# Attention on one core: V products in pairs of key tiles, exponentials per head, and other work between all scores

## The chip, the core and the metric

The kernel runs on one core of a Trainium2 chip. The metric is the device time of the whole program in microseconds, the median of several executions.

## What is computed

The reference is one layer on x of shape (4, 1024, 128): a layer norm, then attention and a gated feed-forward in parallel, both added to x.

```python
xn = _layernorm(x)
# attention: HEADS 16, KV_HEADS 8, DIMS 64, scale = (64 / 16) ** -0.5
xq = rope(q @ Wq); xk = rope(kv @ Wk); xv = kv @ Wv
xk = jnp.repeat(xk, 2, axis=-1); xv = jnp.repeat(xv, 2, axis=-1)
scores = jax.nn.softmax(xq @ xk * scale, axis=-1)
out = (scores @ xv) ... @ Wo
# feed-forward: h = silu(x @ wg.T) * (x @ wu.T); out = h @ wd.T, 384 wide, weights from int
x = x + attn(xn) + ffn(xn)
```

Everything is float32. Since every key and value column is repeated twice, the kernel works with 32 instead of 64 rows per head; for the scores it splits numbers into a rounded part and a rest (`hi`, `lo`), 3 x 32 = 96 rows deep, and takes two more rows for the maximum that is subtracted.

## The kernel before

The feed-forward, the layer norm and the first projections come first, until about 110 us; the rest, which this case is about, is attention. It goes over 4 batches and 4 groups of 4 heads (16 steps), and in each over two halves of the 512 queries: 32 slots, numbered u. Slot u works on four things at once, in program order on each engine, with semaphores between them and no scheduler:

- the scores of slot u: 8 key tiles (kt) of 128 keys, 4 heads (h) each. `score(kt, h)` is one matmul 98 x 512 into `bank_s[:, h % 2]`, so there are two banks, and a score waits for the exponential that read its bank. ScalarE takes the exponential into `prob[:, kt % RING, h]`, a ring of four key tiles. `pv` multiplies a key tile's four heads with V into `bank_o`, four matmuls 32 columns wide, one for each head.
- the row maxima of slot u + 1: 16 tiles, `max_tile` (two matmuls into two of the four `scores` banks), each reduced by VectorE (L824); a tile waits until the reduction of the tile two before has ended. After the 16th, VectorE splits them (`split_max`, the cast L830 and L832), TensorE transposes them, ScalarE reads them and SyncE's queue stores them into the packed queries.
- the projection of slot u + 4 (`project`, four chunks of three matmuls into `scores`, and `project_v`, 12 small matmuls), rotated by VectorE (`rotate`, six operations), rounded by ScalarE and subtracted by GpSimd for slot u + 3 (`round_hi`, `split_lo`). The first two maximum tiles of the next slot wait until the rotation has left the `scores` banks.
- the denominators of slot u - 1 and its output: GpSimd sums the exponentials of key tiles 0 to 6 (`add_probs`, five operations over 2048 elements, L1011 and L1018), VectorE adds tiles 4 and 5 ahead of that (`pair_sum`, L917), in place in `prob`. TensorE multiplies by ones (`denominators`, L404 and L407), transposes (L414), VectorE inverts, ScalarE spreads, TensorE transposes back (L421), VectorE multiplies (`normalise`), TensorE projects with Wo (`project_out`, L430, for slot u - 2), ScalarE reads, GpSimd adds (`add_out`).

Slots 0 to 3 and 28 to 31 are written out, the 24 between are a loop over 4 slots. The last four slots have no projection, the last has no maxima. `prob_ready` counts NE = 3 exponentials for each key tile: heads 0 and 1 together (L768), then 2 and 3 (L779).

Of the kernel before, what the change touches and what calls it, by code (L numbers as in the profile page):

```python
# [69 lines left out]
NE = 3  # L70

EXP_OF = [0, 0, 1, 2]

INVERT_AFTER = 13


def build(nc, x, tables, w_qkv, wo_even, wo_odd, w_gu, w_down, ident_in, out):
# [10 lines left out]
    with ctx:  # L88
# [27 lines left out]
        wgu = keep("wgu", [128, 2, 2 * HT, 128], F32R)  # L116
        wdn = keep("wdn", [128, HT, D])
# [20 lines left out]
        prob_sum = keep("prob_sum", [128, 2, HG, HALF])  # L138

# [208 lines left out]
        def _(pe):  # L348
# [16 lines left out]
            def project_v(w, t, w_from=w_stage, x_from=x_stage):  # L365

                for j in range(QT):
                    at = t * HALF + j * 128
                    for n, (a, r) in enumerate(((0, 0), (1, 0), (0, 1))):
                        last = mm(bank_m[:, j * 128:(j + 1) * 128], x_from[:, r, at:at + 128], w_from[:, a, 4, :],  # L370
                                  start=n == 0, stop=n == 2)
                last.then_inc(proj_ready, 1)
# [159 lines left out]
            def slot(i, j, t, last_pair):  # L532
# [36 lines left out]
                for kt in range(KT):  # L569
                    score(kt, 0)  # L570
                    score(kt, 1)

                    if kt in (0, 3, 4):
                        maxima()
                        pv_before(kt)
                    elif kt < 6:
                        pv_before(kt)
                        maxima()
                    else:
                        if not last_pair:  # L580
                            if kt == 6:

                                pe.wait_ge(max_read, TILES * (v + 1))
                            project(2 * (kt - 6), w, t, s + 2)
                        pv_before(kt)
                    score(kt, 2)
                    if kt in (3, 4):
                        maxima()
                    score(kt, 3)

                    if kt in (0, 1, 2, 3):
                        maxima()
                    if kt == 0:
                        maxima()
                    elif kt == 1:
                        if not is_second(u):
                            project_out(u - 2, 1 - j, s - 1)
                        maxima()
                    elif kt == 2:
                        if not is_first(u):  # L600
                            denominators(u - 1, 1 - t)
                        maxima()
                    elif kt == 4:
                        if not is_first(u):
                            transpose_den(u - 1)
                        maxima()
                    elif kt == 5:
                        if not is_first(u):
                            transpose_inv(u - 1)
                    elif kt == 6:  # L610
                        if do_max:

                            at_least(pe, o_done, u)
                            transpose_max(v)
                        if not last_pair:
                            project(1, w, t, s + 2)
                    elif kt == 7 and not last_pair:
                        project(3, w, t, s + 2)
                        pe.wait_ge(maxT_read, v + 1)
                        project_v(w, t)  # L620
# [6 lines left out]
            pairs_of_steps(pe, body)  # L627
            pv(UNITS - 1, KT - 1, 1)
# [8 lines left out]
        def _(act):  # L637
# [109 lines left out]
            def slot(i, j, t, last_pair):  # L747
# [3 lines left out]
                for kt in range(KT):  # L751

                    if not (first and kt < RING):
                        act.wait_ge(pv_done, 8 * u + kt - 3)
                        if kt == 0:
                            act.wait_ge(sum_done, 5 * u - 1)
                        elif kt == 1:
                            act.wait_ge(pair_done, u)
                        elif kt == 2:
                            act.wait_ge(sum_done, 5 * u)  # L760
                        elif kt == 3:
                            act.wait_ge(den_ready, u)
# [4 lines left out]
                    act.wait_ge(score_ready, 32 * u + 4 * kt + 2)  # L767
                    A(prob[:, kt % RING, 0:2, :], bank_s[:], ACT.Exp).then_inc(prob_ready, 1)  # L768
                    if kt == 0 and not first:
                        read_o(u - 1)  # L770
                    elif kt == 1 and staged:
                        round_hi(0, u + 3, 1 - t, s + 1 + t)
                    elif kt == 2 and not is_second(u):
                        read_y(u - 2)
                    elif kt == 5 and not first:
                        spread_inv(u - 1)
# [3 lines left out]
                    if kt == 0 and not first and staged:  # L780
                        stage_v(u + 3, 1 - t, s + 1 + t)
                    elif kt == 1 and staged:
                        round_hi(1, u + 3, 1 - t, s + 1 + t)
                    elif kt == 2 and not first:
                        read_den(u - 1)
                    elif kt == 6 and not (last_pair and j == 1 and t == 1):
                        read_maxT(u + 1)
# [18 lines left out]
        def _(dve):  # L806
# [150 lines left out]
        def _(pool):  # L957
# [49 lines left out]
            def add_probs(u, t):  # L1007
# [4 lines left out]
                for n, kt in enumerate((2, 3, 4, 6)):  # L1012
# [5 lines left out]
                    TT(prob_sum[:, t], prob_sum[:, t], prob[:, kt % RING], ALU.add).then_inc(sum_done, 1)  # L1018
# [83 lines left out]
```

## Time and profile before

| | us |
|---|---|
| median of 3 runs | 1211.19 |
| lowest, highest | 1210.43, 1213.35 |
| the profiled execution | 1210.01 |
| its span, first to last instruction | 1208.2 |
| TensorE matmul busy | 1161.2 |
| VectorE busy | 892.1 |
| GpSimd busy | 878.2 |
| ScalarE busy | 697.7 |
| mean granted clock of TensorE | 0.989 |

The profiled execution is one run, 1.8 us longer than its span. The chain pieces used below are start to start on the path that ended last; a TensorE piece of several matmuls therefore shows its cost in the pipeline, where the mean of one matmul shows overlap with its neighbours. "x8" behind four V products or four small matmuls counts each of them twice, as the trace does for float32.

### The profile page before, as it was taken

Reading aid. Unit: us, or ns where it says so; the run is one execution under the profiler, and the core shown is the slowest. Engines: PE = TensorE matmul, PEld = TensorE weight load, DVE = VectorE, ACT = ScalarE, POOL = GpSimd, SP = SyncE. Lnnn points to the kernel's source line nnn. Section 1 sums busy time; section 2 is a strip of 40 time slices with the busy share of each in tenths; the row PEclk is TensorE's granted clock in tenths of the full one; section 3 lists DMA queues with packets and bytes.
Section 4 is the critical chain, followed back from the end, with each engine's and each line's share of the span. In section 5 each row is a group of like instructions: output and inputs, shape, how many; then the busy total and the mean of one; then the engine's idle time right before and its main releaser. Section 6 shows DMA issues by size and latency. Waiting matters only on the chain.

```text
span 1208.2 us, 19402 instructions
## 1 busy us (share of the span) xinstructions
PE 1161.2 (96%) x6288; PEld 642.0 (53%) x6288; DVE 892.1 (74%) x1009; ACT 697.7 (58%) x1074; POOL 878.2 (73%) x274
## 2 busy tenths in 40 slices
PE   5898999999999999999999999999999999999985
PEld 4786455555555555555555555555555555554432
DVE  7685778777777778777777777777777777876622
ACT  3333556666666656666666656666666556665563
POOL 2312777887778877787777887787777887787775
PEclk9898999999999999999999999999999999999997
DMA  6652707062421517062422517061422517050000
GB/s 222 172 238 99 213 2 217 1 188 65 142 76 62 156 36 215 0 197 55 141 75 74 143 36 215 0 202 49 148 68 87 131 36 215 0 125 1 4 1 17
DMA packets 56287, 124.58 MB, mean 103 GB/s; under 512 B 7968, under 2 KB 19488, under 8 KB 54048
## 3 DMA queue, kind: packets, MB, share of 16 engines
q1 hardware_dynamic: 56224, 123.89, 35.0%
q8 instruction: 21, 0.34, 0.1%
q14 instruction: 42, 0.34, 0.1%
HBM read 53.08 MB, written 10.49 MB: 53 GB/s over the span
## 4 chain that ended last, share of the span: by engine, by line
PE 90%; DVE 3%; POOL 2%; ACT 1%; issue 1%; DMA 1%; SPq 1%; POOLq 0%; ACTq 0%; DVEq 0%
PE bank_s L542 24%; PE scores L379 22%; PE bank_o L394 20%; PE scores L362 7%; PE bank_m L370 3%; PE bank_m L404 3%; PE bank_m L430 2%; PE bank_m L407 2%; POOL prob_sum L1018 2%; PE scores L480 2%; PE bank_s L497 1%; PE bank_m L414 1%; PE bank_m L421 1%; DVE prob L917 1%; DMA x_all<-x 1%
## 5 line engine op out<-in xcount | busy, mean ns | idle before, releaser
L824 DVE TENSOR_REDUCE row_max<-scores 128x1 f32<-128x1024 f32 x512 | 605.7, 1217 | 194.7 <-PE scores L379 194.7
L1018 POOL TENSOR_TENSOR prob_sum<-prob_sum,prob 128x2048 f32<-128x2048 f32 x128 | 586.3, 4581 | 112.9 <-DVE prob L917 103.8
L542 PE MATMUL bank_s<-qk_pack 98*128 98x512 f32 x1024 | 383.6, 432 | 12.8 <-ACT prob L768 6.7
L779 ACT ACTIVATE prob<-bank_s 128x512 f32<-128x512 f32 x512 | 285.1, 596 | 172.3 <-PE bank_s L542 165.1
L768 ACT ACTIVATE prob<-bank_s 128x1024 f32<-128x1024 f32 x256 | 262.5, 1025 | 187.8 <-PE bank_s L542 180.5
L379 PE MATMUL scores<-qk_pack 96*128 96x512 f32 x1024 | 340.5, 419 | 1.1 <-DVE row_max L824 1.1
L542 PEld LDWEIGHTS bank_s<-qk_pack 98*128 98x128 f32 x1024 | 183.0, 189 | 232.4 <-ACT prob L768 144.3
L394 PE MATMUL bank_o<-prob,v 128*32 128x512 f32 x2048 | 273.6, 606 | 0.9 <-ACT prob L779 0.9
L379 PEld LDWEIGHTS scores<-qk_pack 96*128 96x128 f32 x1024 | 177.0, 190 | 136.8 <-DVE row_max L824 109.1
L963 POOL TENSOR_TENSOR qk_stage<-rope,qk_stage 128x512 fp32r<-128x512 f32 x64 | 82.1, 1283 | 90.8 <-ACT qk_stage L653 90.8
L1011 POOL TENSOR_TENSOR prob_sum<-prob 128x2048 f32<-128x2048 f32 x32 | 146.4, 4575 | 0.0
L362 PE MATMUL scores<-x_stage,w_stage 128*128 128x512 f32 x336 | 100.0, 406 | 0.0
L394 PEld LDWEIGHTS bank_o<-prob,v 128*32 128x32 f32 x2048 | 40.3, 108 | 89.4 <-issue 88.0
L1026 POOL TENSOR_TENSOR y_acc<-y_part,y_acc 128x512 f32<-128x512 f32 x32 | 41.1, 1285 | 56.9 <-ACT y_part L745 56.9
L917 DVE TENSOR_TENSOR prob<-prob 128x2048 f32<-128x2048 f32 x32 | 75.7, 2364 | 0.0
L817 DVE TENSOR_TENSOR rope<-scores,table 128x512 f32<-128x512 f32 x64 | 43.9, 686 | 42.2 <-PE scores L362 42.1
L362 PEld LDWEIGHTS scores<-x_stage,w_stage 128*128 128x128 f32 x336 | 59.4, 189 | 15.2
L734 ACT COPY den<-bank_m 128x512 f32<-128x512 f32 x32 | 18.8, 586 | 52.0 <-PE bank_m L407 52.0
L815 DVE TENSOR_TENSOR scores<-scores,table 128x512 f32<-128x512 f32 x64 | 44.3, 692 | 3.1 <-PE scores L362 2.5
L819 DVE TENSOR_TENSOR rope<-scores,rope 128x512 f32<-128x512 f32 x64 | 44.3, 692 | 2.2
L370 PEld LDWEIGHTS bank_m<-w_stage,x_stage 128*128 128x128 f32 x336 | 41.8, 191 | 2.4
L653 ACT CAST qk_stage<-rope 128x512 fp32r<-128x512 f32 x64 | 39.2, 616 | 4.1 <-DVE rope L819 4.1
(88 smaller groups left out, 679.5 us busy)
## 6 DMA issues: line engine op xcount, KB each, us to landing
qk_pack<-qk_stage SPq DMA_DIRECT2D x384, 128.0 KB, 3.5
table<-tables SPq DMA_DIRECT2D x16, 2048.0 KB, 9.9
w_stage<-w_scratch SPq DMA_DIRECT2D x14, 640.0 KB, 4.7
v<-v_stage SPq DMA_DIRECT2D x32, 256.0 KB, 3.2
xT_scratch<-xT_hl SPq DMA_DIRECT2D x4, 1024.0 KB, 9.5
x_stage<-xT_scratch SPq DMA_DIRECT2D x4, 1024.0 KB, 5.4
w_scratch<-w_split SPq DMA_DIRECT2D x1, 2560.0 KB, 15.1
x_all<-x SPq DMA_DIRECT2D x4, 512.0 KB, 12.5
```

The source lines that it names most:

```text
L362: last = mm(scores[:, c, :], w_from[:, a, c, :], x_from[:, r, cols], start=n == 0, stop=n == 2)
L370: last = mm(bank_m[:, j * 128:(j + 1) * 128], x_from[:, r, at:at + 128], w_from[:, a, 4, :], start=n == 0, stop=n == 2)
L379: last = mm(scores[:, 2 * (m % places) + c, :], qk_pack[n][0:SPLIT_K, 0, t, h, (m % QT) * 128:(m % QT + 1) * 128], qk_pack[n][0:SPLIT_K, 1 ...
L394: last = mm(bank_o[h * E:(h + 1) * E, :], v_sb[n][:, kt, h * E:(h + 1) * E], prob[:, kt % RING, h, :], start=kt == 0, stop=kt == KT - 1)
L542: mm(bank_s[:, h % 2, :], qk_pack[j][0:SCORE_K, 1, kt // QT, h, (kt % QT) * 128:(kt % QT + 1) * 128], qk_pack[j][0:SCORE_K, 0, t, h, :], s ...
L768: A(prob[:, kt % RING, 0:2, :], bank_s[:], ACT.Exp).then_inc(prob_ready, 1)
L779: A(prob[:, kt % RING, h, :], bank_s[:, h % 2, :], ACT.Exp).then_inc(prob_ready, 1)
L824: V.tensor_reduce(row_max[:, m:m + 1], scores[:, at:at + 2, :].rearrange("p c k -> p (c k)"), axis=AX.X, op=ALU.max).then_inc(max_read, 1)
L917: V.tensor_tensor(prob[:, 4 % RING], prob[:, 4 % RING], prob[:, 5 % RING], ALU.add).then_inc(pair_done, 1)
L963: TT(qk_stage[:, 2 * k + 1, t, :], rope[:, 2 * k, :], qk_stage[:, 2 * k, t, :].bitcast(F32), ALU.subtract).then_inc(lo_done, 1)
L1011: TT(prob_sum[:, t], prob[:, 0], prob[:, 1], ALU.add).then_inc(sum_done, 1)
L1018: TT(prob_sum[:, t], prob_sum[:, t], prob[:, kt % RING], ALU.add).then_inc(sum_done, 1)
```

## The change

Three things change in a slot.

- V products are done for two key tiles at once (`pv_pair`), in key tiles 0 (for tiles 6 and 7 of the slot before), 2, 4 and 6.
- Every head has an exponential of its own (NE = 4), and a score waits for the exponential two heads before. ScalarE's other work is placed anew between them; the second `round_hi` stands behind head 1 of key tile 2 instead of behind key tile 1, `read_y` behind key tile 1 instead of inside key tile 2.
- TensorE's other pieces are spread between single scores. Chunk 0 waits for 15 maximum tiles instead of 16. The V projection is done in two halves.

VectorE's sum of key tiles 4 and 5 goes into a buffer of its own, `prob_pair`, and no longer waits for the V product of tile 4; `wgu` and `wdn` share that memory early on. VectorE inverts after maximum tile 9 instead of 13.

```diff
-NE = 3
-EXP_OF = [0, 0, 1, 2]
-INVERT_AFTER = 13
+NE = HG
+INVERT_AFTER = 9
...
+        prob_pair = keep("prob_pair", [128, HG, HALF])
...
-            def project_v(w, t, w_from=w_stage, x_from=x_stage):
-                for j in range(QT):
+            def project_v(w, t, w_from=w_stage, x_from=x_stage, blocks=range(QT)):
+                for j in blocks:
...
-                    at_least(pe, prob_ready, NE * (KT * u + kt) + (EXP_OF[h - 2] + 1 if h > 1 else EXP_OF[h + 2] + 1 - NE))
+                    at_least(pe, prob_ready, NE * (KT * u + kt) + h - 1)
...
-                def pv_before(kt):
+                def pv_pair(kt):
                     if kt > 0:
+                        pv(u, kt - 2, j)
                         pv(u, kt - 1, j)
                     elif not is_first(u):
+                        pv(u - 1, KT - 2, j if t == 1 else 1 - j)
                         pv(u - 1, KT - 1, j if t == 1 else 1 - j)
...
+                def project_chunk(c):
+                    if not last_pair:
+                        pe.wait_ge(max_read, TILES * v + TILES - 1 + c // 2)
+                        project(c, w, t, s + 2)
...
                 for kt in range(KT):
                     score(kt, 0)
...
+                        maxima()
+                        score(kt, 1)
+                        maxima()
+                        score(kt, 2)
+                        pv_pair(kt)
+                        score(kt, 3)
+                        maxima()
                     elif kt == 1:
+                        maxima()
+                        score(kt, 1)
                         if not is_second(u):
                             project_out(u - 2, 1 - j, s - 1)
+                        score(kt, 2)
+                        maxima()
+                        score(kt, 3)
                     elif kt == 2:
+                        maxima()
+                        score(kt, 1)
+                        maxima()
+                        pv_pair(kt)
                         if not is_first(u):
                             denominators(u - 1, 1 - t)
+                        score(kt, 2)
+                        maxima()
+                        score(kt, 3)
+                        maxima()
...
-                        if kt == 0:
-                            act.wait_ge(sum_done, 5 * u - 1)
-                        elif kt == 1:
+                        if kt < 2:
                             act.wait_ge(pair_done, u)
...
-                    A(prob[:, kt % RING, 0:2, :], bank_s[:], ACT.Exp).then_inc(prob_ready, 1)
...
-                    for h in (2, 3):
+                    for h in range(HG):
                         act.wait_ge(score_ready, 32 * u + 4 * kt + h + 1)
                         A(prob[:, kt % RING, h, :], bank_s[:, h % 2, :], ACT.Exp).then_inc(prob_ready, 1)
...
                 dve.wait_ge(prob_ready, NE * (KT * u + 6))
-                dve.wait_ge(pv_done, 8 * u + 5)
-                V.tensor_tensor(prob[:, 4 % RING], prob[:, 4 % RING], prob[:, 5 % RING], ALU.add).then_inc(pair_done, 1)
+                at_least(dve, sum_done, 5 * u - 1)
+                V.tensor_tensor(prob_pair[:], prob[:, 4 % RING], prob[:, 5 % RING], ALU.add).then_inc(pair_done, 1)
```

The order on TensorE from the end of key tile 1 to key tile 3 of slot 2, before (L542 are scores, L379 maximum tiles, L394 V products, L404 and L407 the denominators):

```order
L379 MATMUL scores<-qk_pack 128x512 x2
L542 MATMUL bank_s<-qk_pack 128x512 x2
L394 MATMUL bank_o<-prob,v 32x512 x4
L379 MATMUL scores<-qk_pack 128x512 x2
L542 MATMUL bank_s<-qk_pack 128x512 x2
L379 MATMUL scores<-qk_pack 128x512 x2
L404 MATMUL bank_m<-prob,ones 32x512 x4
L407 MATMUL bank_m<-prob_sum,ones 32x512 x4
L379 MATMUL scores<-qk_pack 128x512 x2
L542 MATMUL bank_s<-qk_pack 128x512 x2
L379 MATMUL scores<-qk_pack 128x512 x2
L394 MATMUL bank_o<-prob,v 32x512 x4
```

and after the change (the same lines are one further down, the transpose L414 is L415):

```order
L543 MATMUL bank_s<-qk_pack 128x512 x2
L380 MATMUL scores<-qk_pack 128x512 x2
L543 MATMUL bank_s<-qk_pack 128x512
L380 MATMUL scores<-qk_pack 128x512 x2
L395 MATMUL bank_o<-prob,v 32x512 x8
L405 MATMUL bank_m<-prob,ones 32x512 x4
L408 MATMUL bank_m<-prob_sum,ones 32x512 x4
L543 MATMUL bank_s<-qk_pack 128x512
L380 MATMUL scores<-qk_pack 128x512 x2
L543 MATMUL bank_s<-qk_pack 128x512
L380 MATMUL scores<-qk_pack 128x512 x2
L543 MATMUL bank_s<-qk_pack 128x512
```

The eight V products of key tiles 0 and 1 stand directly ahead of the denominators, and the maximum tiles that stood around single V products stand between single scores.

ScalarE from the end of the slot before to the denominators of slot 2, before (L768 and L779 exponentials, L728 `read_o`, L658 `stage_v`, L653 `round_hi`, L745 `read_y`, L734 `read_den`):

```order
L768 ACTIVATE prob<-bank_s 128x1024
L728 COPY o_raw<-bank_o 128x512
L779 ACTIVATE prob<-bank_s 128x512 x2
L658 COPY v_stage<-bank_m 128x512
L768 ACTIVATE prob<-bank_s 128x1024
L653 CAST qk_stage<-rope 128x512
L779 ACTIVATE prob<-bank_s 128x512 x2
L653 CAST qk_stage<-rope 128x512
L768 ACTIVATE prob<-bank_s 128x1024
L745 COPY y_part<-bank_m 128x512
L779 ACTIVATE prob<-bank_s 128x512 x2
L734 COPY den<-bank_m 128x512
```

and after the change (L800 exponentials, L761, L691, L686, L778 and L767 the others in the same order of names):

```order
L691 COPY v_stage<-bank_m 128x512
L800 ACTIVATE prob<-bank_s 128x512
L761 COPY o_raw<-bank_o 128x512
L800 ACTIVATE prob<-bank_s 128x512 x2
L686 CAST qk_stage<-rope 128x512
L800 ACTIVATE prob<-bank_s 128x512 x2
L778 COPY y_part<-bank_m 128x512
L800 ACTIVATE prob<-bank_s 128x512 x2
L686 CAST qk_stage<-rope 128x512
L767 COPY den<-bank_m 128x512
L800 ACTIVATE prob<-bank_s 128x512 x8
```

The second `round_hi`, on which GpSimd's chain of the slot waits, stands behind two exponentials of key tile 2, next to the reading of the denominators. The order on GpSimd is the same as before.

## Rows read from the trace of the kernel before

**Rows 1.** The page: busy time, share of the span and instructions.

```profile
PE 1161.2 (96%) x6288; PEld 642.0 (53%) x6288; DVE 892.1 (74%) x1009; ACT 697.7 (58%) x1074; POOL 878.2 (73%) x274
```

**Rows 2.** Chain in order of time, one slot: start us, us, what.

```profile
587.61 0.46 PE scores L379 x2
588.07 1.00 PE bank_o L394 x8
...
593.87 0.89 PE bank_m L430 x8
...
598.31 0.99 PE bank_m L404 x8
599.30 0.86 PE bank_m L407 x8
600.16 0.66 PE scores L379 x2
...
611.79 0.99 PE bank_s L542 x2
...
619.01 0.70 PE scores L362 x3
619.71 1.29 PE bank_m L370 x12
621.00 0.53 PE bank_s L542 x2
621.52 0.46 PE scores L379 x2
```

**Rows 3.** The chain in the last four slots, same columns.

```profile
1095.11 1.03 ACT prob L768
...
1127.50 1.03 ACT prob L768
...
1161.53 0.61 ACT prob L779
...
1162.17 1.01 PE bank_s L542 x2
```

**Rows 4.** Timeline of ScalarE: start us, us, what, [idle before, releaser].

```profile
589.62 1.09 ACT L779 ACTIVATE prob<-bank_s 128x512 f32<-128x512 f32 x2
...
591.30 1.02 ACT L768 ACTIVATE prob<-bank_s 128x1024 f32<-128x1024 f32 x1
```

**Rows 5.** Timeline of VectorE in the slot, and its pair sum in the last slot.

```profile
603.68 3.49 DVE L824 TENSOR_REDUCE row_max<-scores 128x1 f32<-128x1024 f32 x3 [0.47 <-PE scores L379]
...
612.16 0.52 DVE L830 CAST max_hl<-row_max 128x16 fp32r<-128x16 f32 x1
...
613.42 2.28 DVE L917 TENSOR_TENSOR prob<-prob 128x2048 f32<-128x2048 f32 x1
615.62 0.69 DVE L815 TENSOR_TENSOR scores<-scores,table 128x512 f32<-128x512 f32 x1
...
1180.74 4.84 DVE L917 TENSOR_TENSOR prob<-prob 128x2048 f32<-128x2048 f32 x1
```

**Rows 6.** Timeline of GpSimd in the same two stretches.

```profile
594.87 1.29 POOL L963 TENSOR_TENSOR qk_stage<-rope,qk_stage 128x512 fp32r<-128x512 f32 x1 [0.68 <-ACT qk_stage L653]
597.51 1.28 POOL L1026 TENSOR_TENSOR y_acc<-y_part,y_acc 128x512 f32<-128x512 f32 x1 [1.35 <-ACT y_part L745]
598.76 4.58 POOL L1011 TENSOR_TENSOR prob_sum<-prob 128x2048 f32<-128x2048 f32 x1
603.42 9.22 POOL L1018 TENSOR_TENSOR prob_sum<-prob_sum,prob 128x2048 f32<-128x2048 f32 x2
...
1174.17 9.26 POOL L1018 TENSOR_TENSOR prob_sum<-prob_sum,prob 128x2048 f32<-128x2048 f32 x2
```

**Rows 7.** The line of the cast L830: durations in ns min/median/max.

```profile
L830 DVE CAST max_hl<-row_max x32: 175/517/545, 102.5 to 1151.6; 128x16 fp32r<-128x16 f32 x32
```

**Rows 8.** Waits, whole run: who waited for whom, us, times, longest.

```profile
ACT prob L768 <- POOL prob_sum L1018: 4.4, 3, 1.5
```

More of the change, by code:

```diff
@@ L138, in build @@
         prob_sum = keep("prob_sum", [128, 2, HG, HALF])
+        with ExitStack() as early:
+            wgu = keep("wgu", [128, 2, 2 * HT, 128], F32R, early)
+            wdn = keep("wdn", [128, HT, D], F32, early)
+        prob_pair = keep("prob_pair", [128, HG, HALF])
         xn = [v_sb[min(c // 2, 1)][:, c % 2 * QT:(c % 2 + 1) * QT, :] for c in range(CHUNKS)]
@@ L371, in project_v @@
                                   start=n == 0, stop=n == 2)
-                last.then_inc(proj_ready, 1)
+                if j == QT - 1:
+                    last.then_inc(proj_ready, 1)
             def max_tile(v, m, n, t, places=2):
@@ L570, in slot @@
                     score(kt, 0)
[L571 to L592, printed above, removed]
                     if kt == 0:
                         maxima()
+                        score(kt, 1)
[4 more added lines that the diff above has]
+                        maxima()
@@ L600, in slot @@
                         if not is_first(u):
                             denominators(u - 1, 1 - t)
+                        score(kt, 2)
                         maxima()
-                    elif kt == 4:
+                        score(kt, 3)
+                        maxima()
+                    elif kt == 3:
                         if not is_first(u):
                             transpose_den(u - 1)
+                        score(kt, 1)
+                        maxima()
+                        score(kt, 2)
+                        maxima()
+                        score(kt, 3)
+                    elif kt == 4:
+                        maxima()
+                        score(kt, 1)
+                        pv_pair(kt)
+                        score(kt, 2)
+                        maxima()
+                        score(kt, 3)
@@ L609, in slot @@
                             transpose_inv(u - 1)
+                        score(kt, 1)
+                        maxima()
+                        score(kt, 2)
+                        maxima()
+                        score(kt, 3)
                     elif kt == 6:
+                        pv_pair(kt)
+                        score(kt, 1)
+                        project_chunk(0)
+                        score(kt, 2)
                         if do_max:
@@ L614, in slot @@
                             transpose_max(v)
-                        if not last_pair:
[L616 to L620, printed above, removed]
+                        project_chunk(1)
+                        score(kt, 3)
+                        project_chunk(2)
+                    else:
+                        project_chunk(3)
+                        score(kt, 1)
+                        if not last_pair:
+                            pe.wait_ge(maxT_read, v + 1)
+                            project_v(w, t, blocks=range(QT // 2))
+                        score(kt, 2)
+                        if not last_pair:
+                            project_v(w, t, blocks=range(QT // 2, QT))
+                        score(kt, 3)
             def body(i, last_pair):
@@ L627, in _ @@
             pairs_of_steps(pe, body)
+            pv(UNITS - 1, KT - 2, 1)
             pv(UNITS - 1, KT - 1, 1)
@@ L766, in slot @@
                             act.wait_ge(sum_done, 5 * u + kt - 4)
-                    act.wait_ge(score_ready, 32 * u + 4 * kt + 2)
-                    A(prob[:, kt % RING, 0:2, :], bank_s[:], ACT.Exp).then_inc(prob_ready, 1)
[L769 to L776, printed above, removed]
-                    for h in (2, 3):
+                    for h in range(HG):
                         act.wait_ge(score_ready, 32 * u + 4 * kt + h + 1)
                         A(prob[:, kt % RING, h, :], bank_s[:, h % 2, :], ACT.Exp).then_inc(prob_ready, 1)
[L780 to L787, printed above, removed]
+                        if (kt, h) == (0, 2) and not first and staged:
+                            stage_v(u + 3, 1 - t, s + 1 + t)
+                        elif (kt, h) == (0, 3) and not first:
+                            read_o(u - 1)
+                        elif (kt, h) == (1, 1) and staged:
+                            round_hi(0, u + 3, 1 - t, s + 1 + t)
+                        elif (kt, h) == (1, 3) and not is_second(u):
+                            read_y(u - 2)
+                        elif (kt, h) == (2, 1):
+                            if staged:
+                                round_hi(1, u + 3, 1 - t, s + 1 + t)
+                            if not first:
+                                read_den(u - 1)
+                        elif (kt, h) == (4, 1) and not first:
+                            spread_inv(u - 1)
+                        elif (kt, h) == (6, 2) and not (last_pair and j == 1 and t == 1):
+                            read_maxT(u + 1)
             def body(i, last_pair):
@@ L1017, in add_probs @@
                     pool.wait_ge(sum_done, 5 * u + n + 1)
-                    TT(prob_sum[:, t], prob_sum[:, t], prob[:, kt % RING], ALU.add).then_inc(sum_done, 1)
+                    part = prob_pair[:] if kt == 4 else prob[:, kt % RING]
+                    TT(prob_sum[:, t], prob_sum[:, t], part, ALU.add).then_inc(sum_done, 1)
             def add_out(u, t, b):
```

2 lines of the change are left out of this document (removed).

## The prediction

> **What bounds the kernel now.** I read the page's busy shares and the chain that ended last first: TensorE is busy 96% of the span, VectorE 74%, GpSimd 73%, ScalarE 58% [rows 1]. So I went to the chain in order of time for one slot (one half of the queries of one group of heads: 8 key tiles, 4 heads). The slot from 587.61 to 621.52 us is 33.91 us, and every piece of it stands on TensorE [rows 2]. The time to cut is therefore what TensorE does beyond streaming: switches and short stalls.
>
> The free-running prices stand in the same rows: a score or half a maximum tile 0.235 (two in 0.46), a projection chunk 0.70, the V projection 1.29, project_out 0.89, four V products 0.99, and 0.19 more on the piece behind them (0.66 where two such matmuls cost 0.46 elsewhere). The second group of four narrow products, with no wide matmul between, costs 0.86, not 0.99 [rows 2]. Thus going into narrow products costs 0.13 and coming out 0.19, 0.32 together. A slot has 9 such visits: 8 key tiles of V products and the denominators. With 64 score and maximum matmuls (14.95), 4 chunks (2.80), 9 visits (8 x 1.18 + 2.04 = 11.48), project_out (0.89), two transposes (0.88), the maximum's transpose (0.11) and the V projection (1.35 with the 0.06 behind it) that makes 32.45; the other 1.46 us are stalls. The largest is at 611.79: two scores take 0.99 instead of 0.46, since they wait for ScalarE [rows 2].
>
> How a stall arises the last slot shows bare: an exponential runs from 1161.53 for 0.61, and what waited for it starts at 1162.17, two scores in 1.01, each behind a wait [rows 3]. From the end of a score to the start of the next into its bank at least 0.03 + 0.61 + 0.03 + 0.27 = 0.94 us pass (the first 0.03 taken like the second, 0.27 being half of 1.01 less 0.235, what a score takes longer after a wait).
>
> **The change, part by part.**
>
> *V products in pairs.* Four visits go, and a fifth since the pair of key tile 2 now stands directly ahead of the denominators: 5 x 0.32 = 1.60 us a slot off the path. The trace has no eight V products in a row; the nearest row is the second group of the denominators at 0.86. Were the second group as dear as the first (0.99), 0.65 of it would not come. I take 0.86 and keep 0.99 as a bound. The Trainium skill, "TensorEngine Tiling (Array Packing)", section Key Properties, says that changing the tiling mode drains TensorE, while changing only the tile doesn't; by that rule the full 1.60 comes, by the 0.99 bound 0.95.
>
> *V projection in halves.* One more boundary of 0.06; the work is the same.
>
> *Exponentials per head.* Two exponentials of 0.60 take 1.09, so they overlap by 0.11 and have a pitch of 0.49; one over two heads takes 1.02, with the same overlap 0.91 [rows 4]. ScalarE now pays 8 x 4 x 0.49 = 15.7 us a slot against 8 x (0.91 + 2 x 0.49) = 15.1, and it is idle four tenths of the time. What it buys is that a score's bank is free 0.94 after it, not after two heads. But "a piece behind every score" fails at three ends of key tiles and at the end of the slot: behind heads 3 of tiles 1, 3, 5 and 7 comes the next tile's head 0 at once. Two scores of one bank are then only 0.47 + 0.235 = 0.70 apart, so 0.24 is missing, unless something else has stalled before.
>
> *Other stalls, walked from the rows.* I walk one slot from its first score at 0.
> - Head of the slot: score (0,1) comes 0.70 after score (7,3) ended, stall 0.2.
> - Key tile 1: ScalarE has six operations at 0.49 (4 exponentials, a rounding, read_y) in a stretch in which TensorE needs 2.8 us; score (2,0) waits 0.25. The maximum tile just ahead of the pair in key tile 2 waits 0.15 for the reduction two before.
> - Key tiles 2 and 3: after the pair and the denominators VectorE has been idle for nearly 3 us, then gets tiles at 0.7 us distance. Its pitch is 1.16 (three in 3.49) [rows 5]. Tile 7 starts at 13.4, is reduced from 13.9, the reduction of tile 8 ends at 16.3, tile 10 can start at 16.6, TensorE was ready at 16.2: 0.4, and 0.2 for tile 11. The same at tile 15 in key tile 5: 0.4.
> - End of the slot. The rounding of the second rotated half moves from behind key tile 1 to behind head 1 of key tile 2. It ends at 10.3, GpSimd subtracts until 11.65 (1.29), add_out until 12.9 (1.28), then three sums of 4.6: the third ends at 26.9. In the slot of before the same ends are at 596.16, 598.79 and 612.64, that is 9.1, 11.7 and 25.6 from its first score at 587.09 (33.91 ahead of the one at 621.00) [rows 2, 6]. The last reduction now ends near 26.0, and the cast behind it (L830) takes 0.52 in the trace where 0.175 is its least [rows 5, 7]: it starts at 612.16 and ends within 0.05 us of the end of GpSimd's sum. In the last slot the pair sum takes 4.84 instead of 2.28: it starts at 1180.74, GpSimd's sums run until 1183.43, and 2.15 us later it is done [rows 5, 6]. So these VectorE operations, SBUF to SBUF, wait for a running GpSimd operation to end. The cast now waits 0.9 instead of 0.35; normalise (0.6), pair sum (2.25) and six rotation steps (0.69 each, 0.63 to 0.73 apart) end near 34.0, that is 1.1 into the next slot, and the second maximum tile, which waits for them, can start at 1.4 where TensorE is ready at 1.1: 0.3.
>
> The Trainium skill, "SBUF — State Buffer", section Terms, says that VectorE and GpSimd arbitrate for one port pair, locked for a full instruction, and that the loser fully blocks. The trace agrees at 1180.74. With it the walk ends at 32.86, without the lock at 32.6, 8 us less in all.
>
> The stalls add up to 1.95 with the rounding of the walk. The same walk over the slot of before gives 33.67 instead of 33.91, so 0.24 escapes it, and I add that. Slot: 32.45 - 1.60 + 0.06 + 1.95 + 0.24 = **33.10**, against 33.91: 0.81 less. The gain is the switches (1.54) less half of it lost to more stalls (0.7). 28 slots have this form: **22.7 us**.
>
> *The last four slots* have no projections. There ScalarE waits some 1.5 us for GpSimd, three times [rows 8], at the first exponential of a slot, because the pair sum is written over key tile 4 and GpSimd reads it there; from one such exponential to the next it is 32.4 (1095.11 to 1127.50 [rows 3]), and so once more. Now the pair sum has a buffer of its own, and the first exponential waits only for VectorE. The next limit is the loop exponential (2,0), tiles 2 to 5, pair sum, two GpSimd sums (9.27), exponential (2,0), 30.7 by the same walk. Twice 1.7 is 3.4, 0.3 for the one before. In the last slot, without maxima, a key tile takes 1.03 + 0.50 + 0.61 + 1.01 and four or five hops of 0.03, 3.3 [rows 3]; per head it would be 2 x (0.94 + 0.235) = 2.35, plus that part of a pair of V products that nothing covers, some 0.7 a tile: 8 x 0.25, 2.1 us in all.
>
> Sum: 22.7 + 0.3 + 3.4 + 2.1 = 28.5 us. The profiled execution took 1210.01 for a span of 1208.2, 1.2 below the median of 1211.19. From the median: **1182 to 1183, I say 1182.**
>
> **Hidden work.** The new buffer's wait (the GpSimd sum that read it last) ended 20 us earlier. Exponential (0,h) waits for the pair sum, done at 30.1, slot end 33.1: 3 us of cover. Exponential (4,0) waits for GpSimd's first sum, done at 17.5; it is wanted at 17.9: 0.4 of cover. Exponential (2,0) waits for GpSimd's last sum of the slot before (39.4 less 33.1 = 6.3, wanted at 8.2): 1.9. Chunk 0 needs tile 14 read: more than 2 us of cover, since the last pair stands ahead. SP's packs start later by at most the 3 us by which the rounding moved, and end before the maximum's pack at the slot's end.
>
> **Rivals.**
> 1. The second group of a pair costs 0.99. For: each V product group in the trace costs that; against: the denominators' 0.86. 5 x 0.13 x 32 = 21 us lost, but stalls of VectorE shrink as the pair grows: about 1195.
> 2. GpSimd decides, slower than before. Its chain from the moved rounding to the first sum has only 0.4 us before exponential (4,0), and each 1 us that its third sum comes later holds cast, pair sum and rotations, and the next slot's second maximum tile, by 1 us. It turns slower when GpSimd is over 0.8 us later than walked. At 1.1 us: +0.3 x 28, near 1220 with exponential (4,0) late too. For: the cast already touches GpSimd's end in every steady slot. Against: two of its sums take 9.22 in one row and 9.26 in another [rows 6].
> 3. The stalls of scores and maxima eat the whole gain, within 0.3% of 1211: needs 1.5 us of stalls more than before, twice the 0.7 walked. TensorE would then show 0.86 for second groups and the same 33.9 a slot.
> 4. The lock bites less, or the 0.24 doesn't recur: 32.6 to 32.8 a slot, near 1172.
>
> **Chances.** Mine 0.55 (1175 to 1190), rival 1 0.13, rival 2 0.10, rival 3 0.10, rival 4 0.12. A change of 0.3% (3.6 us) is about what a measurement of this kernel can tell. Faster 0.82 (mine, 1, 4 and part of 3), same 0.08, slower 0.10. The range leaves out rival 2 and half of 3: 1168 to 1203.
>
> **What the profile after would show.** Chain: eight V products in 1.85 (else 1.98: rival 1), four visits a slot; slot period 33.1 and 30.7 in the last four; maximum tiles of key tiles 3 and 5 waiting for the row maximum; the cast near 0.9 (over 1.8: rival 2); no wait of ScalarE for GpSimd. It is wrong if ScalarE waits for GpSimd's sum at key tile 4, or if scores wait inside key tiles and not at their ends.

## The result, and the profile after

The changed kernel takes 1203.97 us (median of 20, 1195.12 to 1210.51), the kernel before on the same chips 1211.77 (median of 20, 1209.72 to 1213.35): a ratio of 0.9936, 95% interval 0.9923 to 0.9948. It is faster, clear of noise but by under 1%: 7.8 us, a quarter of the 28.5 that were forecast, and 1 us above the range. Its runs spread over 15 us, those of before over 4.

The page of after, busy shares, and the shares of the chain by engine:

```profile
PE 1138.4 (95%) x6288; PEld 669.7 (56%) x6288; DVE 886.1 (74%) x1009; ACT 733.7 (61%) x1330; POOL 876.5 (73%) x274
...
PE 69%; DVE 8%; SPq 8%; issue 7%; DMA 4%; ACT 2%; POOL 1%; DVEq 0%; POOLq 0%; ACTq 0%
```

TensorE is 23 us less busy than in [rows 1], and its share of the chain fell from 90% to 69%; SyncE's queue (SPq) and "issue" rose there from 1% each. The chain in order of time over a plain slot (start us, us, what), against [rows 2]:

```profile
593.60 1.85 PE bank_o L395 x16
595.45 0.86 PE bank_m L405 x8
596.31 0.86 PE bank_m L408 x8
597.17 0.43 PE bank_s L543
...
599.25 1.23 DVE row_max L854
600.47 0.04 issue
600.52 0.72 PE scores L380 x2
...
615.19 0.62 PE bank_m L370 x6
615.81 0.28 PE bank_s L543
616.09 0.62 PE bank_m L370 x6
616.71 0.56 PE bank_s L543 x2
617.28 0.47 PE scores L380 x2
617.75 0.45 PE bank_s L543
```

Eight V products take 1.85, and the denominators behind them 0.86 each: the pairs pay as forecast. The chain goes through VectorE's reductions behind them, as walked. But the slots are not alike. The cast L860 runs once in a slot; its rows in VectorE's timeline (start us, us) show the periods:

```profile
472.68 0.74 DVE L860 CAST max_hl<-row_max 128x16 fp32r<-128x16 f32 x1
...
505.35 0.73 DVE L860 CAST max_hl<-row_max 128x16 fp32r<-128x16 f32 x1
...
540.01 0.76 DVE L860 CAST max_hl<-row_max 128x16 fp32r<-128x16 f32 x1
...
577.45 0.74 DVE L860 CAST max_hl<-row_max 128x16 fp32r<-128x16 f32 x1
...
610.10 0.77 DVE L860 CAST max_hl<-row_max 128x16 fp32r<-128x16 f32 x1
```

From one to the next it is 32.67, 34.66, 37.44 and 32.65 us. All 31 periods, as differences of such starts, here of before, of after and of four of the experiments:

```
period     0     1     2-4   5     8     12    13    16    20    21    24    others   29    30
before     35.8  33.6  33.8  33.9  33.9  33.9  33.9  34.0  33.9  33.9  33.9  33.9     32.4  32.4
after      32.5  36.0  32.6  35.9  36.3  34.7  37.4  36.4  36.4  37.2  36.5  32.65    33.8  32.2
e1         31.3  38.0  32.6  35.4  32.7  32.6  36.6  33.0  32.6  37.5  32.6  32.6     33.8  32.2
e2         31.3  37.9  32.6  32.6  39.7  36.0  32.6  37.9  37.4  32.7  38.0  32.6     32.2  33.5
e7         34.4  33.4  34.0  34.0  37.4  36.0  34.0  38.9  37.4  34.0  39.0  33.9     31.7  31.4
e9         31.3  37.9  32.6  32.7  32.6  32.6  32.6  33.0  32.6  32.6  32.7  32.6     30.8  30.7
```

A plain slot is 32.65, less than the 33.10 forecast. Periods 2 to 28 gain 27 x (33.88 - 32.65) = 33.2 us, and eight long ones among them give 29.6 back. These are of two kinds: 8, 12, 16, 20 and 24 hold a jump of the loop over four slots (17.0 us above 32.65), and 5, 13 and 21 a load of a batch's x (12.6); period 1 holds such a load too (36.0). The rest of the 6.5 us between the two profiled spans lies at the ends: periods 0 and 1 together gain 0.9, the last two lose 1.2, behind the last maxima 3.9 come off, and 1.0 is lost ahead of the first period.

**The jump.** The chain of after at such a place:

```profile
649.37 0.30 PE bank_s L543
...
649.69 0.04 ACT prob L800
...
649.76 0.04 ACTq L197
649.80 2.52 issue
652.33 0.06 ACTq L197
...
652.57 0.60 ACT prob L800
...
653.22 0.50 PE bank_s L543
653.72 2.98 PE bank_o L395 x16
656.70 0.73 PE bank_s L543
```

L197 is the loop. ScalarE's sequencer reaches the branch at 649.76, while the last exponential of the round runs, and goes on at 652.33: 2.52 us in which it waits for nothing that the trace shows (2.35 to 2.60 at the five jumps). Between the exponentials ScalarE is idle for 2.28. The kernel before has this too; its chain at the same place:

```profile
653.02 0.04 ACTq L197
653.06 0.15 issue
653.21 0.59 ACT prob L779
653.80 1.84 issue
655.65 0.06 ACTq L197
...
655.91 1.03 ACT prob L768
```

The stop is as long there: from the branch at 653.02 to 655.65 it is 2.6 us, as from 649.76 to 652.33 after the change. The row has 1.84 because the last exponential ran during the first part of it, and ScalarE is idle for 2.10. But there the V projection (1.29) and the first scores lay behind the last exponential, and ScalarE was idle then in every slot (1.67 at the slot that begins at 485, without a jump); the period is 33.98. After the change the last score is the last piece of the slot, and head 2 of the next waits for the exponential of its head 0, behind the stop. The Trainium skill, "Runtime: NRT & Kernel Launch", section Instruction fetch mechanics, says that a taken branch whose target isn't in the prefetched pages makes execution wait for a fetch. The trace shows the stop and its place, not the fetch.

The stop costs more than its length. Busy time of each engine and the granted clock (the column PEclk, as a share of full speed) in stretches of 4 us of after around it:

```profile
core 0: us, PE busy (x) PEld busy (x) DVE busy (x) ACT busy (x) POOL busy (x), PEclk, DMA share, GB/s
645.00:649.00 4.00, 4.00 (x25) 3.43 (x23) 3.96 (x6) 2.72 (x6) 2.29 (x1) 1.00 0.02 6
649.00:653.00 4.00, 2.31 (x11) 1.40 (x10) 3.72 (x5) 1.41 (x3) 3.92 (x2) 1.00 0.01 4
653.00:657.00 4.00, 3.78 (x18) 1.07 (x19) 0.00 (x0) 1.73 (x4) 2.91 (x1) 0.66 0.01 2
657.00:661.00 4.00, 4.00 (x20) 3.08 (x20) 2.70 (x3) 3.38 (x7) 0.76 (x1) 0.91 0.76 153
```

TensorE was busy for 2.31 of 4 us, and in the next 4 the granted clock averages 0.66, part of the time at the lower level of 1.2 GHz. Eight V products take 2.98 instead of 1.85 and the score behind them 0.73 instead of 0.43. I estimate what the clock takes as the missing share of full speed times the length of the stretch: 4 x (0.34 + 0.09) = 1.7 us here. The jump of period 12 shows the stop without it (same columns):

```profile
512.00:516.00 4.00, 2.28 (x8) 1.24 (x7) 3.28 (x4) 1.60 (x3) 3.92 (x2) 1.00 0.01 4
516.00:520.00 4.00, 4.00 (x27) 2.18 (x27) 1.06 (x1) 2.68 (x7) 2.50 (x1) 1.00 0.10 12
```

TensorE was idle just as long and the clock stayed at full speed. That period is 34.66, 2.0 above a plain one; the other four, each with 1.7 us of missing clock, are 3.7 to 3.8 above. So a jump costs 2.0 us by the wait and, where the clock falls, 1.7 by the clock.

**The x load.** The chain of after ahead of period 13's slow slot:

```profile
545.28 0.60 SPq L241
...
546.02 2.25 DMA qk_pack<-max_rows
548.27 0.24 issue
548.51 0.79 PE bank_s L543
...
551.86 3.57 PE bank_o L395 x16
```

In one step of four SyncE loads x as well, and its step (loads, 26 transfers, then the store of the maxima) is one chain. SyncE's timeline of before, same step:

```profile
541.21 7.75 SPq L235 DMA_DIRECT2D qk_pack<-qk_stage  x12
549.00 0.60 SPq L241 DMA_DIRECT2D v<-v_stage  x1
549.74 33.25 SPq L246 DMA_DIRECT2D qk_pack<-max_rows  x2
```

(The last row holds two stores, one slot apart.) In both it stores the maxima right behind the last transfer. In the kernel before that landed about 1.2 us ahead of the next slot's first score (549.74 + 2.3 against 587.09 - 33.9 = 553.2). The change took from both ends: slots are 1.2 us shorter, and the step begins later, for it waits for the V product of the slot's last key tile (`pv_done`, L302: SyncE waits 67.9 us in all for TensorE there, 47.6 before), which moved from behind the second score of a slot to behind the third, and there behind the four products of key tile 6. The trace of e1 below, which has no jump in the way, shows the sum: the x load is issued at 512.07, some 4.1 us behind the slot's first score (before, 521.68, 2.4 behind), and the chain from there to the landing of the maxima takes 30.8 (30.4 before); that is 34.9, 2.3 more than a plain slot, and with 1.7 us of missing clock behind it the 4.0 by which its period 13 is long. In after, the jump at the start of the same slot puts the load off further, to 518.40, 6.1 behind, in a slot that is itself 2.0 longer. TensorE then waits, and here too the clock falls, to 0.56 and 0.58 in the 8 us from 548: 3.57 for eight V products.

### The profile page after: what moved, and what is told of

Read it like the earlier page. It is cut to its first block, busy times and chain, and to the rows that moved or that the text cites. A ratio compares the mean times of both kernels' runs of the same rounds, so it can differ in the third digit from the quotient of the medians.

```text
span 1201.7 us, 20113 instructions
## 1 busy us (share of the span) xinstructions
PE 1138.4 (95%) x6288; PEld 669.7 (56%) x6288; DVE 886.1 (74%) x1009; ACT 733.7 (61%) x1330; POOL 876.5 (73%) x274
## 3 DMA queue, kind: packets, MB, share of 16 engines
q1 hardware_dynamic: 56224, 123.89, 35.4%
## 4 chain that ended last, share of the span: by engine, by line
PE 69%; DVE 8%; SPq 8%; issue 7%; DMA 4%; ACT 2%; POOL 1%; DVEq 0%; POOLq 0%; ACTq 0%
PE bank_o L395 19%; PE bank_s L543 16%; PE scores L380 15%; DVE row_max L854 7%; PE scores L362 6%; SPq L235 6%; PE bank_m L370 3%; PE bank_m L431 2%; PE bank_m L408 2%; PE bank_m L405 2%; ACT prob L800 2%; DMA x_stage<-xT_scratch 2%; PE scores L481 2%; PE bank_s L498 1%; DMA x_all<-x 1%
## 5 line engine op out<-in xcount | busy, mean ns | idle before, releaser
L854 DVE TENSOR_REDUCE row_max<-scores 128x1 f32<-128x1024 f32 x512 | 597.7, 1215 | 237.2 <-PE scores L380 235.9
L800 ACT ACTIVATE prob<-bank_s 128x512 f32<-128x512 f32 x1024 | 595.6, 600 | 288.1 <-PE bank_s L543 246.4
L543 PE MATMUL bank_s<-qk_pack 98*128 98x512 f32 x1024 | 434.1, 440 | 24.9 <-ACT prob L800 15.7
L1049 POOL TENSOR_TENSOR prob_sum<-prob_sum,prob 128x2048 f32<-128x2048 f32 x96 | 439.1, 4574 | 9.3 <-ACT prob L800 0.5
L543 PEld LDWEIGHTS bank_s<-qk_pack 98*128 98x128 f32 x1024 | 194.7, 191 | 217.1 <-ACT prob L800 96.7
L395 PE MATMUL bank_o<-prob,v 128*32 128x512 f32 x2048 | 260.3, 628 | 0.0
L1049 POOL TENSOR_TENSOR prob_sum<-prob_sum,prob_pair 128x2048 f32<-128x2048 f32 x32 | 147.0, 4595 | 105.9 <-DVE prob_pair L947 105.9
L395 PEld LDWEIGHTS bank_o<-prob,v 128*32 128x32 f32 x2048 | 55.0, 112 | 127.2 <-issue 71.9
L767 ACT COPY den<-bank_m 128x512 f32<-128x512 f32 x32 | 18.7, 586 | 91.9 <-PE bank_m L408 91.9
L947 DVE TENSOR_TENSOR prob_pair<-prob 128x2048 f32<-128x2048 f32 x32 | 73.8, 2307 | 1.4 <-ACT prob L800 1.4
L370 PE MATMUL bank_m<-w_stage,x_stage 128*128 128x128 f32 x336 | 43.8, 266 | 0.0
```

What stands on the lines that cost most here:

```text
L395: last = mm(bank_o[h * E:(h + 1) * E, :], v_sb[n][:, kt, h * E:(h + 1) * E], prob[:, kt % RING, h, :], start=kt == 0, stop=kt == KT - 1)
L543: mm(bank_s[:, h % 2, :], qk_pack[j][0:SCORE_K, 1, kt // QT, h, (kt % QT) * 128:(kt % QT + 1) * 128], qk_pack[j][0:SCORE_K, 0, t, h, :], s ...
L854: V.tensor_reduce(row_max[:, m:m + 1], scores[:, at:at + 2, :].rearrange("p c k -> p (c k)"), axis=AX.X, op=ALU.max).then_inc(max_read, 1)
L947: V.tensor_tensor(prob_pair[:], prob[:, 4 % RING], prob[:, 5 % RING], ALU.add).then_inc(pair_done, 1)
L1049: TT(prob_sum[:, t], prob_sum[:, t], part, ALU.add).then_inc(sum_done, 1)
```

## The experiments

The theory: a plain slot gains what was forecast and more, and the change gives 30 us of it back at two kinds of places, where ScalarE stands at the loop's jump and where SyncE's transfers are late behind an x load; each is to be had back by itself. Against it stand that the long slots come from the pairs themselves (a heavier load, a lower clock, whatever the code around it), and that the gain in plain slots is not the pairs' but that of the exponentials per head.

All times are medians; ratios are against the kernel before on the same chip, with 95% intervals. "e9" and the like name the kernels.

**e1: the loop written out** (no jump between slots, on TensorE, ScalarE, VectorE and GpSimd).

```diff
-            with eng.Fori(1, STEPS // 2 - 1) as i:
+            for i in range(1, STEPS // 2 - 1):
```

> The changed kernel with slots 4 to 27 written out on TensorE, ScalarE, VectorE and GpSimd instead of a loop over 4 slots. Theory A (ScalarE's 2.5 us stop at the loop's jump is no longer covered, TensorE then runs empty and at the lower clock): the five slots with a jump fall from 34.7 to 36.5 us to the 32.65 of the others, 17 us in all, to about 1187; the slots with an x load stay long (35.9 to 37.4). Rival B (these slots are long because of SyncE's queue or the clock alone): no change, 1204. Rival C (code written out is fetched while it runs and stops every few slots): some slots elsewhere grow, the sum stays near 1204 or above.

1186.42 us, 0.9795 (0.9777 to 0.9812). The five jump periods are 32.6 to 33.0, the x load periods stay at 35.4 to 38.0. Theory A holds, to 1 us; B and C fall. ScalarE's waits of "issue" are gone from the list, and the runs spread over 5 us instead of 15.

**e2: SyncE loads before it waits for the V products.**

```diff
-                if not (last_pair and n == 1):
-                    at_least(sp, pv_done, 16 * s)
...
                     sp.wait_ge(v_staged, 2 * s + 3)
+                    at_least(sp, pv_done, 16 * s)
                     pack_half(1 - n, 0)
...
-            with sp.Fori(1, B - 1) as b:
+            for b in range(1, B - 1):
```

> The changed kernel, but SyncE waits for the V products of the slot before only ahead of the packs, not ahead of the loads of x, weights and tables (and its loop over batches is written out with constants). Theory: in the four steps that load x the loads and 26 transfers of the step are one chain that ends with the store of the maxima; begun some 3 us earlier it costs the first slot of the next half 3 us less each, 12 us in all of the 16 that these four slots are long: about 1192, the waits of TensorE for the packed maxima (7.7 us) near 0. Rival: the chain is held by the landing of the x load or by the DMA engines, not by its start: within 2 us of 1204.

1199.83 us, 0.9905 (0.9877 to 0.9932). Periods 5, 13 and 21 fall to 32.6 and 32.7: the mechanism holds, and the rival falls with it. The whole doesn't show it: the interval overlaps that of the changed kernel (0.9923 to 0.9948), and the sum is 8 us short of the forecast. Period 1 is as long as in e1 (37.9), and the jump periods are longer in its profile (36.0 to 39.7). Of that the missing clock is 5.1 us at period 8, none at 12 and 1.7 at the others; at all five TensorE also waits once more behind the jump, and why stays open.

**e3: the second half of the V projection behind the slot's last score.**

```diff
                         score(kt, 2)
+                        score(kt, 3)
                         if not last_pair:
                             project_v(w, t, blocks=range(QT // 2, QT))
-                        score(kt, 3)
```

> The changed kernel with the second half of the V projection behind the last score of a slot, not ahead of it. In a plain slot nothing should change (32.65). At the loop's jumps ScalarE's last exponential ends 0.6 to 0.9 us earlier against TensorE, so its stop of 2.5 us costs TensorE 0.9 us less, and perhaps the lower clock behind it: 4 to 12 us in all, 1192 to 1200. Rival B (the jump isn't the cause): 1204.

1198.06 us, 0.9875 (0.9838 to 0.9912), in the expected range. In its profile three of the jump periods are 34.0 to 34.2 and two 35.6 and 35.7. At the three the granted clock stays at 1.00, at the two 1.7 us of it are missing; so part of the gain is that the clock fell at two jumps here and at four in after. The wait itself costs 1.5 to 1.7 over a plain period instead of 2.0. The plain ones are 32.5, 0.1 shorter than forecast.

**e7: the pairs undone**, all else as changed: V products singly behind or between the scores of their old key tile.

```diff
-                        pv(u, kt - 2, j)
                         pv(u, kt - 1, j)
...
                             project_out(u - 2, 1 - j, s - 1)
                         score(kt, 2)
+                        pv_one(kt)
```

The added line stands in key tile 1, and likewise in 3, 5 and 7; `pv_pair` is named `pv_one`, and the last product behind the loop goes.

> The changed kernel with the V products of one key tile at a time (in the tile's place behind it, as before the change) and everything else as changed: the pairs undone. By the price of a visit, 5 x 0.32 us a slot: a plain slot of 32.65 becomes 34.2 if no stall shrinks, 33.8 if half of the stalls are covered by the V products that now stand in key tiles 1, 3, 5 and 7. The whole 1235 to 1245 if the long slots stay as long. Rival (pairing brings nothing by itself, the single pieces between scores do): a plain slot stays within 0.4 of 32.65 and the whole within 12 of 1204.

1225.41 us, 1.0114 (1.0095 to 1.0133). A plain slot is 33.8 to 34.0, as long as before the change. So the exponentials per head and the single pieces between scores bring nothing to it as long as the V products stand singly, and undoing the pairs costs the whole 1.3 us, within the expected range of 1.15 to 1.55. The rival falls. Pairs alone, in the kernel before, were not run: whether they would bring the 1.3 us without the other two parts is not shown. The whole is 10 us under the expected 1235 to 1245, since not all long slots stayed long: the x load periods are 34.0. Slots are longer here, and the V product that SyncE waits for no longer has the four of key tile 6 ahead of it. The jump periods are long here too (36.0 to 39.0). They follow the clock: 36.0 with none of it missing, 37.4 twice with 1.7 us, 38.9 and 39.0 with 3.4 (the same estimate over stretches of 2 us).

**e9: e1 and e2 together.**

> The changed kernel with the slots written out and SyncE's loads ahead of its wait for the V products (e1 and e2 together). Theory: the two causes are separate, so the five jumps (17 us) and the three x loads of batches 1 to 3 (some 11 us) go together: 31 of 32 slots at 32.65 or so, about 1174. Rival (one cause, such as late packs after any disturbance): no better than 1184 to 1187.

1169.36 us, 0.9659 (0.9637 to 0.9680), 5 us better than expected. Only period 1 is long. The last two are 30.8 and 30.7, as the prediction had them, 4.6 us less than in after: that is the difference.

**e10: e9, single V products in key tiles 6 and 7 of the last four slots, and SyncE's wait for the early stores moved to their first reload.**

```diff
                     elif kt == 6:
-                        pv_pair(kt)
+                        if last_pair:
+                            pv(u, kt - 2, j)
+                        else:
+                            pv_pair(kt)
...
                         project_chunk(3)
+                        if last_pair:
+                            pv(u, kt - 2, j)
...
-            for n in range(4):
-                sp.wait_ge(y_saved[n], 16 * len(range(n, CHUNKS, 4)) - (16 if n < 2 else 0))
...
+                    if b == 1:
+                        for m in range(4):
+                            sp.wait_ge(y_saved[m], 16 * len(range(m, CHUNKS, 4)) - (16 if m < 2 else 0))
                     sp.wait_ge(y_added, 2 * s)
```

> As e9, and in the last four slots the V products of key tiles 4 and 5 stand singly in key tiles 6 and 7, and SyncE waits for the stores of the feed-forward's output only ahead of their first reload, not ahead of the first step. Theory: the slot with index 1 (38.0) loses some 4 us, since its chain begins with that store; the last slots lose the empty 1 to 2 us and the lower clock behind them, 2 to 3 us: about 1168. Rival: the first step is bound by the x load itself and the lower clock comes anyway: within 2 us of e9.

1166.39 us, 0.9624 (0.9606 to 0.9641): period 1 falls from 37.9 to 33.9. It is the fastest version. The last periods don't change (30.9 and 30.5, together as in e9); in e9 there was no lower clock to save in them, and there the expectation was wrong. The last slot got longer: behind the last maxima e10 takes 55.0 us of its span, e9 52.7. Up to the end of the last GpSimd sum e10 is 0.4 faster, and behind it 2.6 slower: the clock is 0.50 to 0.52 there (1151 to 1163), and 1.00 over the same work in e9. So in these two profiles the single V products are no gain, and what e10 gains is SyncE's earlier start; that edit alone was not run.

**e11: the edits of e9 on the kernel before.**

> The kernel of before with the same two edits as e9 (slots written out, loads ahead of the wait). Theory: before the change ScalarE's stop at the jump and the x loads are covered, so neither edit has anything to take: within 3 us of the kernel before. The first slots may lose up to 2 us. Rival (the edits are good by themselves, whatever the order of the work): 20 us or more faster, like the changed kernel.

1208.08 us, 0.9975 (0.9963 to 0.9988), 2.5 us. The edits are worth some 34 us in the changed kernel and next to nothing in the kernel before: both costs were covered there.

**e12: e9 with the second rounding back behind key tile 1.**

```diff
-                        elif (kt, h) == (1, 3) and not is_second(u):
-                            read_y(u - 2)
+                        elif (kt, h) == (1, 3):
+                            if staged:
+                                round_hi(1, u + 3, 1 - t, s + 1 + t)
+                            if not is_second(u):
+                                read_y(u - 2)
```

> As e9, with the second rounding (round_hi of the other half) back behind key tile 1, where GpSimd's chain starts 2 us earlier and VectorE's cast no longer waits for GpSimd's sum (0.76 back to 0.18 to 0.5). By the walk of the prediction, in which the second maximum tile waits for the rotations behind that cast, a plain slot loses 0.3: 8 us, 1166. By the trace of the changed kernel the rotations end just in time and nothing waits: within 2 us of e9.

1171.53 us, 0.9674 (0.9652 to 0.9697), the same as e9 within the intervals. VectorE's timelines, first of e9, then of e12:

```profile
595.86 0.87 DVE L858 CAST max_hl<-row_max 128x16 fp32r<-128x16 f32 x1
```

```profile
595.26 0.17 DVE L859 CAST max_hl<-row_max 128x16 fp32r<-128x16 f32 x1
```

In e9 the cast ends at 596.73 and the running GpSimd sum at 596.69; in e12 that sum is over at 594.70, before the cast starts. The cast's wait for GpSimd is gone, and a plain slot is still 32.6. The wait is real and costs a plain slot nothing.

## Why the prediction was wrong

- **The switches**: right. 1.85 and 0.86 in the rows of after; rival 1 (0.99) is out.
- **The stalls of a plain slot**: too high by 0.45. The walk's places are in the trace (0.22 at the second score, the reductions behind the denominators). Two terms were not: the 0.3 at the second maximum tile, since the rotations end just in time (e12 shows that it is no wait), and the 0.24 that I carried over from the walk of before. This miss helped: 27 x 0.45 = 12 us. Had the plain slot been the 33.10 of the forecast, the long periods would have left nothing of the gain, so a ratio below 1 owes something to luck.
- **"28 slots have this form"**: this step failed. I priced one plain slot and multiplied, and put the cost of the loop's jump and of the x load at nothing; they measured 17.0 and 12.6 us. The slots with the loop's jump and with the x load were plain before only because slack covered them, and the change used that slack up. Of the jump the trace of before had the row (1.84 of "issue" on ScalarE at 653.80, the end of a stop of 2.6), and I didn't look at what covered it: ScalarE's idle time at the end of a slot, which the new order of scores removed. For SyncE I checked a plain step ("end before the maximum's pack"), not the one that loads x, where 1.2 us was left, and I priced the later start of its packs by the moved rounding, not by `pv_done`.
- **Exponential (0,h), (4,0), (2,0)**: the covers held; ScalarE never waits for GpSimd. Rival 2 is out.
- **The last four slots**: 66.0 for the last two periods instead of 61.4. The loop through GpSimd is 30.7 as forecast, in e9 and e12. In after and e1 the first of the two is 33.8, the second 32.2. In after the granted clock falls in both (columns as above):

```profile
1084.00:1088.00 4.00, 3.15 (x9) 1.15 (x7) 2.87 (x3) 3.72 (x8) 1.05 (x1) 0.98 0.02 4
1088.00:1092.00 4.00, 4.00 (x11) 2.23 (x15) 2.38 (x2) 2.19 (x4) 3.86 (x2) 0.50 0.02 4
1092.00:1096.00 4.00, 4.00 (x22) 1.46 (x15) 0.35 (x2) 0.75 (x2) 4.00 (x1) 0.67 0.00 0
...
1120.00:1124.00 4.00, 3.66 (x9) 2.28 (x10) 0.75 (x2) 3.11 (x6) 3.92 (x1) 0.74 0.07 20
1124.00:1128.00 4.00, 4.00 (x24) 1.54 (x23) 1.77 (x3) 1.41 (x4) 3.86 (x2) 0.83 0.00 0
```

  By the estimate above 3.3 us of clock are missing in the first and 1.7 in the second, and these periods are 3.1 and 1.5 longer than in e9, where the code on TensorE is the same and the clock stays at 1.00 up to the last maxima. So the path was right and the clock, which the sum had at full speed, was the term that it lacked. Why it fell in the one and not in the other stays open.

  Behind the last maxima 3.9 us came off, for 2.1 forecast. Not all of it is the change. The eight matmuls of the last output projection, in TensorE's timeline of before and of after:

```profile
1200.79 2.07 PE L430 MATMUL bank_m<-wo_stage,o_norm 128*128 128x128 f32 x8 [0.78 <-DVE o_norm L927]
```

```profile
1195.15 1.16 PE L431 MATMUL bank_m<-wo_stage,o_norm 128*128 128x128 f32 x8 [0.78 <-DVE o_norm L957]
```

  In before the granted clock is 0.50 there, in after 1.00, and from the last denominators to GpSimd's last addition it is 7.4 instead of 5.4 us: 2.0 of the 3.9 are clock. The other 1.9 are the change together with what the clock took earlier in that slot of after (0.76 and 0.81 in the 8 us from 1154, 1.7 by the estimate); the change by itself would then be 3.6, more than forecast.
- **Rival 3** (the stalls eat the gain, needing 1.5 us more a slot) had the right size in sum and the wrong place: nothing in plain slots, 2 to 5 us in each of nine others.

Left open: why the clock falls behind one stop and not behind another of the same length, and whether that makes the spread of after from run to run (only one of its runs was profiled; within it, and in e3 and e7, the clock is what the jump periods differ by); and what TensorE waits for behind the jumps in e2.

## What to carry to other kernels

- Price the rare slots by themselves: the one with the loop's jump, with a batch's load, the first and last. A change that tightens the plain slot takes their cover away, and here eight periods gave back nine tenths (29.6 of 33.2 us) of what 27 had gained.
- Around a loop's jump keep work behind the last instruction of each engine that the others wait for, or write the loop out where code size allows.
- Group matmuls of one tiling: a switch in and out is 0.32 us here, and grouping them was worth 1.3 us in a plain slot of 33.9.
- Before one place is explained by its code, look at the granted clock there: the same stop cost 2.0 us or 3.7, and two versions differed by 2 us at their very end.

## What the runs showed of the hardware

- A stretch of 4 us in which TensorE was busy 2.31 was followed by one with a granted clock of 0.66, and eight V products took 2.98 instead of 1.85; behind the late maxima of a batch's x load they took 3.57. A stretch with 2.28 was followed by 1.00: the same idle time didn't always bring the clock down.
- ScalarE's stop at the jump of a loop, from its branch to the next round: 2.6 us in the kernel before, 2.35 to 2.60 after. There is none in the loop written out, where the body stands six times over; one period was 0.3 us longer than a plain one there, the others not.
- VectorE's cast of 128 x 16 elements takes 0.17 alone and 0.87 when a GpSimd sum is running; it ended 0.04 us after the sum.
